# Two GNN layers on one core: messages in tiles of 128 nodes, one of four P rows added by VectorE, and an update moved ahead in the last stage

## What is computed

```python
h = relu(layernorm(x))                                  # 3125 x 256
messages = (h[src] + edge_emb[type]) @ msg_W + msg_b
delta = tanh(gelu([h[src], h[dst], e, task] @ att_W1 + att_b1) @ att_W2 + att_b2)
w = 1 + edge_scale * delta
agg = segment_sum(modulated(messages) * w, dst) / max(segment_sum(w, dst), 1)
updated = gelu([h, modulated(agg)] @ up_W1 + up_b1) @ up_W2 + up_b2
x = x + layernorm(h + updated) * ln_g + ln_b
```

## Time and profile before

| | |
|---|---|
| median of 3 runs | 1305.84 us (1302.63 to 1306.84) |
| profiled execution, its own time | 1307.77 us |
| its span, first to last instruction | 1305.8 us |
| mean granted TensorE clock | 0.798 of full speed |
| busy over the span: TensorE, VectorE, GpSimd, ScalarE | 72%, 69%, 64%, 46% |
| edge loop, 900 to 1100 us: TensorE, VectorE, GpSimd | 200.0, 171.6, 150.3 us of 200 |
| indirect DMAs of the edge loop | 418, 946 to 949 ns each |

### The profile page before, as it was taken

One profiled execution on the slowest core, in us unless ns is written; L12 is line 12 of the kernel. 1 busy time (PEld: TensorE's weight loads), 2 busy tenths in 40 slices (PEclk: granted clock), 3 DMA queues, 4 the chain that ended last, 5 costly groups with the idle time before them and its releaser, 6 DMA issues. The chain is left out here.

```text
span 1305.8 us, 18685 instructions
## 1 busy us (share of the span) xinstructions
PE 937.8 (72%) x5019; PEld 728.9 (56%) x5019; DVE 899.9 (69%) x2594; ACT 605.0 (46%) x1479; POOL 831.5 (64%) x868
## 2 busy tenths in 40 slices
PE   7505455664123511389899999999999999999985
PEld 6402233332112510277677777777777777777774
DVE  6477575665566544345656888888888888888658
ACT  6433333433243433223325665566666656556544
POOL 0377777777777777663127777777777777777012
PEclk9855555555555555589899999999999999999988
DMA  5568666566776666544357777877877787887312
GB/s 157 133 201 279 220 214 216 201 224 221 241 261 232 201 204 216 191 116 130 69 152 231 235 234 235 241 235 234 238 239 236 232 236 241 234 235 237 99 38 85
DMA packets 100774, 263.58 MB, mean 202 GB/s; under 512 B 21094, under 2 KB 42117, under 8 KB 94530
## 3 DMA queue, kind: packets, MB, share of 16 engines
q0 software_dynamic: 53856, 164.87, 42.7%
q1 hardware_dynamic: 45026, 95.76, 22.1%
q10 hardware_dynamic: 1792, 1.75, 0.5%
HBM read 192.92 MB, written 68.25 MB: 200 GB/s over the span
## 5 line engine op out<-in xcount | busy, mean ns | idle before, releaser
L675 POOL DMA_INDIRECT gath<-hp_d,chain_src x391 | 370.8, 948 | 169.3 <-issue 166.3
L1353 POOL DMA_INDIRECT gbuf<-pm_d,srcs x350 | 332.1, 949 | 108.5 <-issue 104.1
L922 DVE SCALAR_TENSOR_TENSOR hist<-hist,smask,ps 128x256 f32<-128x256 f32 x390 | 186.7, 479 | 194.8 <-ACT ps L716 186.8
L716 ACT ACTIVATE ps<-gath,chain_w 128x256 f32<-128x256 f32 x391 | 164.6, 464 | 312.9 <-DMA gath<-hp_d,chain_src 295.1
L1750 DVE TENSOR_TENSOR acc<-ps,acc 112x272 f32 x418 | 183.7, 439 | 69.2 <-DVE acc L1750 64.0
L1596 ACT ACTIVATE ps<-ps 128x512 f32<-128x512 f32 x210 | 122.1, 582 | 191.7 <-PE ps L1492 191.6
L1492 PE MATMUL ps<-gbuf,ident 128*128 128x256 f32 x700 | 210.1, 382 | 0.0
L1490 PE MATMUL ps<-qw,halves 128*128 x1254 | 206.6, 274 | 2.3 <-DVE qw L1699 2.3
L1516 PE MATMUL ps<-gbuf,placed 128*112 128x272 f32 x700 | 175.4, 393 | 1.0 <-ACT placed L1615 0.7
L837 PE MATMUL ps<-win_hot,node_hot 128*112 128x28 bf16 x391 | 43.7, 253 | 175.2 <-DVE win_hot L1009 175.2
L1490 PEld LDWEIGHTS ps<-qw,halves 128*128 128x128 bf16 x1254 | 122.9, 98 | 73.8 <-issue 6.9
(11 more groups left out here) (292 smaller groups left out, 1384.2 us busy)
## 6 DMA issues: line engine op xcount, KB each, us to landing
hist_d<-hist SPq DMA_DIRECT2D x48, 1024.0 KB, 4.6
gath<-hp_d,chain_src POOLq DMA_INDIRECT x391, 3.1
wn<-node_row_d SPq DMA_DIRECT2D x26, 224.0 KB
key<-node_row_d SPq DMA_DIRECT2D x26, 224.0 KB, 3.5
gbuf<-pm_d,srcs POOLq DMA_INDIRECT x350, 4.0
pm_d<-gbuf SPq DMA_DIRECT2D x6, 896.0 KB, 5.1
hb_d<-gbuf SPq DMA_DIRECT2D x7, 448.0 KB, 3.2
qw<-hb_d SPq DMA_DIRECT2D x7, 448.0 KB, 8.4
```

What stands on the lines that cost most here:

```text
L675: eng.indirect_dma_start(row_at(j), None, hp_d[:, :], bass.IndirectOffsetOnAxis(ap=chain_src[:, j:j + 1], axis=0)).then_inc(got[q % RINGG] ...
L716: eng.activation(weighted_at(j), row_at(j), ACT.Copy, scale=chain_w[:, j:j + 1]).then_inc(gw_ready, 1)
L922: eng.scalar_tensor_tensor(out=state_at(j), in0=state_at(j - 1) if j else first_state[:, :], scalar=smask[:, j:j + 1], in1=weighted_at(j), ...
L1353: eng.indirect_dma_start(gath3(g % RING)[:, k, 0:2 * D], None, pm_d[:, :], bass.IndirectOffsetOnAxis(ap=srcs[:, g * SG + k:g * SG + k + 1] ...
```

## The change

It has three parts.

1. **Messages.** The turned columns in `up` are laid out as two planes of 3136 nodes (`nodes`), so that `messages` can cut them into 25 tiles of 128 nodes (the last has 64) without regard to windows. The groups get 3, 4, 3, 4, 3, 4 and 4 tiles (`tiles_of`). VectorE's copy to `up` becomes two instructions, one for each plane.
2. **Edge loop.** In each full group the identity product of the fourth slot is left out. VectorE adds the gathered P row to z in PSUM instead, after it has compared the keys, once all of z is there (`z_ready`). ScalarE's gelu of the second half waits for that add (`p_added`).
3. **Last stage.** VectorE runs `update(1)` before `rows_y(0)` and `shifts(0)`, not after them.

```diff
+            def nodes(n0, n1, half):
+                return up[:, half * NT * WIN + n0:half * NT * WIN + n1]
...
+            def tiles_of(i):
+                first, last = i * GN * WIN // P, (i + 1) * GN * WIN // P
+                return range(first, last if i < NG - 1 else -(-NM // P))
...
+            def p_by_vector(g, k):
+                return slots_in(g) == SG and k == SG - 1
@@ TensorE, messages @@
-                    for k in ks:
-                        if i >= 1 and k >= 2:
-                            eng.wait_ge(pm_a if k == 2 else pm_v, 2 * i)
-                        at = (i * GN + k) * ACW0
+                    for k, m in enumerate(tiles_of(i)):
+                        if i >= 1 and k == 2:
+                            eng.wait_ge(pm_a, by_act(i))
+                        if i >= 1 and k == 3:
+                            eng.wait_ge(pm_v, by_vec(i))
+                        n = nodes_in(m)
@@ TensorE, edge_step @@
-                                eng.matmul(to, hot[g % 2][:, k * P:(k + 1) * P],
-                                           qw[:, bass.ds(w[k] * (3 * D) + part * D, D)], start=part == 0, stop=False)
-                            ins = eng.matmul(to, ident[:, :], gath3(r)[:, k, 0:D], start=False, stop=True)
+                                ins = eng.matmul(to, hot[g % 2][:, k * P:(k + 1) * P],
+                                           qw[:, bass.ds(w[k] * (3 * D) + part * D, D)], start=part == 0,
+                                           stop=part == 2 and p_by_vector(g, k))
+                            if not p_by_vector(g, k):
+                                ins = eng.matmul(to, ident[:, :], gath3(r)[:, k, 0:D], start=False, stop=True)
@@ ScalarE, edge_step @@
                             eng.wait_ge(z_ready, g * 2 + half + 1)
+                            if half == 1 and slots_in(g) == SG:
+                                eng.wait_ge(p_added, g + 1)
@@ VectorE, message stage @@
-                    eng.tensor_copy(up[:, i * GN * ACW0:(i + 1) * GN * ACW0].rearrange("p (k c) -> p k c", k=GN),
-                                    bank(4, 2).rearrange("p (k c) -> p k c", k=GN)[:, :, 0:ACW0]).then_inc(hT_ready, 1)
+                    for hf in range(2):
+                        ins = eng.tensor_copy(nodes(i * GN * WIN, (i + 1) * GN * WIN, hf).rearrange("p (k n) -> p k n", k=GN),
+                                              bank(4, 2).rearrange("p (k c) -> p k c", k=GN)[:, :, hf * WIN:(hf + 1) * WIN])
+                    ins.then_inc(hT_ready, 1)
@@ VectorE, edge_step, between match_keys(g + 1) and the products with w2b @@
+                    if has(g) and slots_in(g) == SG:
+                        eng.wait_ge(z_ready, g * 2 + 2)
+                        zk = bank(2 * (g % 2), 2)[:, (SG - 1) * D:SG * D]
+                        eng.tensor_tensor(zk, zk, gath3(r)[:, SG - 1, 0:D], ALU.add).then_inc(p_added, 1)
@@ VectorE, last stage @@
                 update(0)
+                update(1)
                 rows_y(0)
                 shifts(0)
-                update(1)
```

More of the change, by code:

```diff
@@ L1162, in gnn_two_layers @@
             gath = [gbuf[:, r * SG * SW:(r + 1) * SG * SW] for r in range(RING - 1)] + [attw[:, :]]
-            pm = [gbuf[0:WIN, r * GN * 2 * D:(r + 1) * GN * 2 * D] for r in range(2)]
+            pm = [gbuf[:, r * GN * 2 * D:(r + 1) * GN * 2 * D] for r in range(2)]
             h, hb, ngb = ([gbuf[0:WIN, (4 + 2 * n + r) * GN * D:(5 + 2 * n + r) * GN * D] for r in range(2)] for n in range(3))
@@ L1238, in early_bank, with pair_cols, nodes_in, by_act @@
                 return bank(4 + p % 3)
-            def pair_cols(p):
-                return up[:, p * 2 * ACW0:(p + 1) * 2 * ACW0].rearrange("p (k h n) -> p k h n", k=2, h=2)
+            def nodes(n0, n1, half):
+                return up[:, half * NT * WIN + n0:half * NT * WIN + n1]
+            def pair_cols(p, half):
+                return nodes(p * 2 * WIN, (p + 1) * 2 * WIN, half).rearrange("p (k n) -> p k n", k=2)
+            NM = NT * WIN
+            def tiles_of(i):
+                first, last = i * GN * WIN // P, (i + 1) * GN * WIN // P
+                return range(first, last if i < NG - 1 else -(-NM // P))
+            def nodes_in(m):
+                return min(P, NM - m * P)
+            def by_act(i):
+                return sum((len(tiles_of(n)) + 1) // 2 for n in range(i))
+            def by_vec(i):
+                return sum(len(tiles_of(n)) // 2 for n in range(i))
             def slots_in(g):
                 return min(SG, USED - g * SG)
+            def p_by_vector(g, k):
+                return slots_in(g) == SG and k == SG - 1
             def gath3(r):
@@ L1266, in pm_parts @@
             def pm_parts(i):
-                return [(0, GN)] if i < NG - 1 else [(0, 2), (2, 3), (3, 4)]
+                return [(0, len(tiles_of(i)))] if i < NG - 1 else [(0, 2), (2, 3), (3, 4)]
+            assert len(tiles_of(NG - 1)) == GN and max(len(tiles_of(i)) for i in range(NG)) <= GN
             def put_all(eng):
@@ L1286, in _ @@
                     for k0, k1 in pm_parts(i):
[L1287 to L1291, removed]
+                        eng.wait_ge(pm_a, by_act(i) + (k1 + 1) // 2)
+                        eng.wait_ge(pm_v, by_vec(i) + k1 // 2)
+                        m0, m1 = tiles_of(i)[k0], tiles_of(i)[k1 - 1] + 1
+                        n = nodes_in(m1 - 1)
+                        eng.dma_start(pm_d[m0 * P:(m1 - 1) * P + n, :].rearrange("(k p) d -> p k d", p=n),
+                                      rows_by_k(pm[i % 2])[0:n, k0:k1, :]).then_inc(pm_out[i % 2], 16)
                     if i == REC_AT:
@@ L1419, in keys_q @@
                     for k in range(GN):
[L1420 removed]
+                        at = (i * GN + k) * WIN
                         for hf in range(2):
[L1422 removed]
+                            ins = eng.matmul(q_bank(i)[0:WIN, k * D:(k + 1) * D], nodes(at, at + WIN, hf),
                                              attw[:, (2 + hf) * D:(3 + hf) * D], start=hf == 0, stop=hf == 1)
@@ L1452, in _ @@
                         turn_n(i + 2)
-                    messages(i, range(GN))
+                    messages(i)
                     if i + 2 < NG:
@@ L1467, in own_early @@
                             ins = eng.matmul(early_bank(p)[:, f * ACW0:(f + 1) * ACW0], upw1[:, hf * D + f * P:hf * D + (f + 1) * P],
-                                             pair_cols(p)[:, :, hf, :], start=hf == 0, stop=hf == 1)
+                                             pair_cols(p, hf), start=hf == 0, stop=hf == 1)
                     ins.then_inc(u_ready, 1)
```

41 lines of the change are left out of this document (24 added, 17 removed).

## The result

The changed kernel takes 1333.73 us in the median of 4 runs (1331.38 to 1334.7), the kernel before, timed beside it, 1305.73 (1302.63 to 1306.84). The ratio is 1.0216, with a 95% interval of 1.0193 to 1.0238. It is slower by 2.2%, where 1.2% was forecast: 1322 us was 12 too low, inside the range of 1312 to 1345. All that follows compares the profiled execution of the change (own time 1334.7 us, span 1332.9) with that of before (1307.77, 1305.8): 27.1 us more between first and last instruction.

What follows compares the result with a forecast made beforehand. Edge loop bound by TensorE, GpSimd and VectorE together, VectorE without room for an add. 1307.77 + 28.9 (loop) - 4.8 (messages) - 8.4 (last stage) = 1323.5 us, so 1322 in the median; range 1312 to 1345.

Steps and rivals of the forecast that it cites:

- The bound: Edge loop: TensorE without idle, GpSimd 5.00 and VectorE 4.94 us, all within 2% of the 5.024 us step.
- The rival in which TensorE sets the end: Edge loop: VectorE has room and its gaps shrink, GpSimd sets 5.00 us a step; 1290 us in the median; chance 0.07.
- The add itself, 0.34 us: Edge loop: the new add takes 0.34 us of VectorE's step, with its result there after 0.42.
- The 0.65 us that stood as the upper end: Edge loop: highest cost of the add on VectorE, read from an accumulation and its gap.
- The round trip, 0.03 us: Edge loop: VectorE's third product stalls 0.03 us a step for ScalarE's gelu, which waits for the add.
- The rival of a dearer hand-over: Edge loop: VectorE to ScalarE takes 0.21 us, stall 0.23, step 5.51, 1342 us in all; chance 0.16.
- The own share "falls into their new slack": Edge loop: every eleventh group's own-share product fits into the new slack of TensorE and ScalarE.
- The message stage, 4.8 us less: Message stage: three fewer tiles save 5.16 us on TensorE, the copy in two parts costs 0.35.
- The last stage, 8.4 us less: Last stage: moving the update saves 8.4 us, 5.4 of it TensorE's idle and the rest the clock.
- The rival of 1358 us: Edge loop: TensorE's clock falls in its new idle, 36 us if in a tenth of the steps; chance 0.04.
- The savings do not arrive: Message and last stages: other waits replace the tiles and the clock stays low, 1329 us; chance 0.08.
- the likeliest range of 1316 to 1332: Whole kernel: range around the main case, with a stall of 0 to 0.1 and 3 us either way for the clock.

Runs made afterwards that it cites:

- e10: Changed kernel with VectorE's add moved ahead of the key comparison, both ScalarE waits kept; 1324.24 us, ratio 1.0121 to the kernel before.
- e11: Changed kernel with ScalarE's gelu of the second half waiting for the add alone, no longer also for z; 1326.08 us, ratio 1.0148 to the kernel before.
- e12: Kernel before with only the add on VectorE in place of the identity product, run on an undisturbed chip; 1343.95 us, ratio 1.0273.
- e8: Changed kernel with the add only in the nine own-share groups, ahead of the key comparison, identity product elsewhere; 1289.5 us, ratio 0.9876 to the kernel before.
- e9: Changed kernel with the identity product back and the add and its wait removed; 1293.7 us, ratio 0.9908 to the kernel before.
- e7: Changed kernel with neither product nor add for the fourth slot, so its result is incomplete; 1286.82 us in one run.
- e2: Kernel before with only the add on VectorE in place of the identity product, on the chip with pauses; 1532.3 us, ratio 1.0037.
- e6: Kernel before with only the message tiles of 128 nodes, on the chip with pauses; 1525.31 us, ratio 0.998.
- e5: Kernel before with only the second update moved ahead of the first rows, on the chip with pauses; 1522.59 us, ratio 0.9968.

## Why the forecast was right, and where not

**The bound.** Right. VectorE's step of 4.94 us was the one thing that could not be added to, and its apparent 28 us of spare time could not be used. The rival in which TensorE sets the end (1290 us) is refuted: no 0.21 us gap of the accumulations shrank, and all three still name VectorE's own accumulation as the releaser.

**The add itself, 0.34 us.** Right to 0.01: 903.77 - 903.44 = 0.33 here, 0.34 in the next step, and 5.27 - 4.94 = 0.33 in `e10`. That it writes to PSUM costs nothing on VectorE. The 0.65 us that stood as the upper end came from a row that has its own wait, and the add has none of that kind. By the rule of the Trainium skill that the forecast weighed (VectorE: DVE Perf Modes, "The DRAIN you can't avoid") the step of `e10` would have been 5.36 (an estimate, 4.94 + 0.42). The trace does not agree with it here either. That section of the Trainium skill has an exception, though, which the forecast left out: a next instruction that is not held starts earlier. This the trace agrees with, 0.33 us after the start of one that lasts 0.42.

**The round trip, 0.03 us: this is the step that failed.** The forecast took "each hand-over takes about 0.03 us" from the earlier trace rows, a case where ScalarE had a single wait. In the change it has two in a row, and the hand-over took 0.10 by the rows. The first two products covered only 1.02 us, so all that came on top was stall: 0.11, not 0.03, 101 times 0.08 = 8.1 us. `e11` shows it by taking the first wait away: 0.04 for the hand-over, 0.05 of stall, a step of 5.33 to 5.34, close to the forecast's 5.31. The mechanism was named rightly and was mis-sized. The rival of a dearer hand-over had it at 0.21 and a step of 5.51; the truth lay between the two.

**What lies between the steps.** 101 steps of 5.39 to 5.40 are 544.4 to 545.4 us, and 546.8 were measured. The rest, some 2 us, is six steps of 5.63 to 5.76, four of them with a second row like this in VectorE's timeline of the changed kernel:

```profile
922.10 0.44 DVE L1788 TENSOR_TENSOR acc<-ps,acc 112x272 f32 x1 [0.21 <-DVE acc L1788]
923.10 0.44 DVE L1788 TENSOR_TENSOR acc<-ps,acc 112x272 f32 x1 [0.56 <-DVE acc L1788]
```

The gap is 0.56 us, not 0.21, and no view shows what holds VectorE: the releaser named had been done for 0.35 us by then. VectorE's timeline of the kernel before has six such rows too, always 16 steps apart (12, 28 and so on to 92), this one, of step 44, among them:

```profile
920.43 0.44 DVE L1750 TENSOR_TENSOR acc<-ps,acc 112x272 f32 x1 [0.58 <-DVE acc L1750]
```

The forecast started from VectorE's step of 4.94, to which these pauses come on top, and left them out. It took 28.9 as 101 times 5.31 less 507.4. With 8.1 for the larger stall and the 2.4 that 546.8 has over 544.4 it is 39.4, all of what the loop gained.

**The own share "falls into their new slack".** Right. In the kernel before, VectorE's step behind each of these nine groups takes 5.4 to 5.6 us instead of 4.94, as VectorE stands before the third product for ScalarE's late gelu. The last row is one of them (0.59 us of idle). In the changed kernel none of these nine steps is longer than the others. This for the most part, the six pauses for the rest, and not a shortage in each step, made the pace before 5.024 rather than 4.94.

**The message stage, 4.8 us less.** 2.4 arrived. The size was nearly right, and part of it was given back by the clock. TensorE's timeline of the changed kernel, from the first turn of h to the first product of the loop:

```profile
574.28 0.98 PE L1421 MATMUL ps<-ident,gbuf 112*128 112x112 f32 x8 [0.89 <-ACT gbuf L1564]
...
603.98 0.96 PE L1399 MATMUL ps<-ident,gbuf 112*128 112x112 f32 x8 [1.70 <-DVE placed L1730]
604.95 1.81 PE L1435 MATMUL ps<-attw,up 128*128 128x256 f32 x4
...
643.38 2.08 PE L1435 MATMUL ps<-attw,up 128*128 128x256 f32 x4 [1.73 <-DVE up L1746]
...
697.43 0.82 PE L1516 MATMUL ps<-qw,halves 128*128 x3 [2.35 <-DVE qw L1735]
```

At full clock four of these products take 1.03 us; 1.81 and 2.08 are rows at the lower level (1.2 GHz, not 2.4). It fell three times, at 605, 622 and 643 us, before only at 643, but there for twice as long as each of the three. The stage's length goes with the mean granted clock. By the same two instructions, and the windows view between them:

| kernel | tiles | falls | mean granted clock | stage, us |
|---|---|---|---|---|
| before; `e12` | 112 | 1; 1 | 0.97; 0.97 | 125.56; 125.67 |
| `e8` | 128 | 1 | 0.97 | 121.28 |
| `e9`; `e11` | 128 | 2; 2 | 0.97; 0.97 | 121.93; 121.83 |
| changed; `e7` | 128 | 3; 3 | 0.96; 0.96 | 123.15; 123.40 |
| `e10` | 128 | 3 | 0.95 | 124.71 |

At the same granted clock 125.6 becomes 121.3 to 121.9: some 4 us less, with 4.8 forecast. More time at the lower level takes part of it back. So the tiles do pay, though no run with the tiles alone on an undisturbed chip shows it in its time. What decides about a fall stays open. TensorE's timeline of `e8` at the place of the first fall:

```profile
603.60 0.96 PE L1402 MATMUL ps<-ident,gbuf 112*128 112x112 f32 x8 [1.70 <-DVE placed L1733]
604.57 1.13 PE L1438 MATMUL ps<-attw,up 128*128 128x256 f32 x4
605.54 1.03 PE L1438 MATMUL ps<-mc,up 128*128 128x256 f32 x4
```

The same idle of 1.70 us, the same products after it, and no fall. The forecast read from the earlier trace rows that an idle of 1.69 is harmless, because the turning after it still took 0.96. That one row showed nothing: at the same idle the clock falls in some executions and not in others.

**The last stage, 8.4 us less.** 9.3 were measured. TensorE's timeline of the changed kernel, against the earlier trace rows:

```profile
1278.11 3.62 PE L1926 MATMUL ps<-upw,u 128*112 128x256 f32 x16
1281.56 1.94 PE L1916 MATMUL ps<-dg,acc 128*128 128x112 f32 x16
...
1284.23 3.62 PE L1926 MATMUL ps<-upw,u 128*112 128x256 f32 x16
...
1315.64 3.68 PE L1926 MATMUL ps<-upw,u 128*112 128x256 f32 x16 [2.38 <-ACT u L1977]
```

and VectorE's rows of groups 1 and 2:

```profile
1287.95 1.22 DVE L2008 TENSOR_TENSOR y_c<-ps,qw 112x1024 f32<-112x1024 f32 x1 [0.43 <-PE ps L1926]
...
1294.67 1.21 DVE L2008 TENSOR_TENSOR y_c<-ps,qw 112x1024 f32<-112x1024 f32 x1
```

The idle of 5.39 us is gone, and so are the slow rows behind it: the update takes 1.94 us in place of 3.73, the rows 3.62 in place of 4.25. The last stage begins 36.4 us later than before, so 1287.95 answers to 1251.5, where 1251.9 was forecast and 1260.29 had been. From there the pace is 1294.67 - 1287.95 = 6.72, as before (6.73). Near the end the two differ by the clock once more, after the same idle: the last rows take 3.68 us, those of before, ahead of which TensorE had idled 2.39 us as well, 5.33:

```profile
1287.99 5.33 PE L1884 MATMUL ps<-upw,u 128*112 128x256 f32 x16 [2.39 <-ACT u L1935]
```

`e9` has the same 65.7 us for its last stage. With the move it takes 65.7 to 66.4 us in ten traces, without it 73.0 to 75.0 in four (before, `e2`, `e6`, `e12`). So the move is worth some 7 to 9 us, and the 9.3 are its upper end, as the kernel before had the lower clock at its last rows.

**The clock in the loop.** The rival of 1358 us is refuted. TensorE idles, by 0.55 us where it waits for the keys (0.9 was forecast), and the granted clock of 900 to 1100 us stays 1.00. The to and fro of the clock that the Trainium skill describes (TensorE: Matmul & The Clock Gate, "A second HAM failure mode: psum-queue depth-cycling") did not occur here, with an idle of this size in most steps; the falls of the message stage came after idles of 1.7 to 1.8 us.

**The savings do not arrive** (1329 us): they did, 11.7 of 13.2 us. The time came near that figure for another reason.

**Range and chances.** 1333.73 is outside the likeliest range of 1316 to 1332, since its stall went only up to 0.1, and inside the full one, which the dearer hand-over had widened.

## What to carry to other kernels

Before giving an in-order engine one more instruction, follow one of its steps through the timeline: a busy share of 86% was an engine with no time to spare, and the work taken from TensorE was worth 0.07 us a step on average, and VectorE paid 0.45 for it. When the new instruction hands its result to another engine and gets an answer back, put work between the two, and let the receiver wait once, for the last event alone. And spend such a shift only on the steps in which the relieved engine is really late: nine adds were worth more than 104.

## What the runs showed of the hardware

- A second wait in a row on ScalarE costs, even when the first has long been met: with two, the gelu started 0.09 to 0.10 us after the end of VectorE's result, in each of 104 adds; with one, 0.03 to 0.04.
- A `tensor_tensor` of 128x256 fp32 that reads and writes PSUM lasts 0.42 us on VectorE, and the next instruction starts 0.33 to 0.34 after it, as after one that writes to SBUF.
- After an idle of 1.70 us at the same place (near 604 us) TensorE's clock fell in three of the kernels with tiles of 128 (changed, `e7`, `e10`) and did not in the other three (`e8`, `e9`, `e11`); the message stage took 121.3 us at a mean granted clock of 0.97 and 124.7 at 0.95.
- On one chip every kernel, the one before among them, ran 14 to 18% longer, with engines standing still for microseconds, ScalarE in one place of `e5` for 7.08 us on a result that was there. A step without such a pause was as exact there as elsewhere (4.94, 5.27, 5.33, 5.39), so a cause could be read from single steps where the medians misled: there the add seemed to cost 0.4%, on the other chip it was 2.7%.
